# Attention with P times V of two steps in a row, a sixth buffer of exponentials, and scores and merged pieces ordered by array half

## The chip, the cores and the metric

One core of one Trainium2 chip. The metric is the device time of the whole kernel in microseconds, the median of the runs. The core's engines work side by side, each through its own list of instructions in order, and wait for each other on semaphores: TensorE (PE; its weight loads are PEld), VectorE (DVE), ScalarE (ACT), GpSimd (POOL) and SyncE (SP), which issues most DMAs. Matmuls write to PSUM, which has 8 banks of 128 x 512 float32.

## What is computed

Three stages on x of 4 x 1024 x 128: a feed-forward block with 8 experts, causal attention with 16 heads of 8 dimensions over 4 key heads, and the feed-forward block again. The change touches the attention alone:

```python
def _L0_attn_ref(qkv, Wq, bq, Wk, bk, Wv, bv, Wo, bo, slopes):
    ...
    scores = jnp.einsum('bhgqd,bhkd->bhgqk', qg, k) * scale
    rel = jnp.arange(S)[None, :] - jnp.arange(S)[:, None]
    bias = slopes.reshape(KVH, G, 1, 1) * rel
    causal = jnp.tril(jnp.ones((S, S), dtype=bool))
    bias = jnp.where(causal, bias, -jnp.inf)
    attn = jax.nn.softmax(scores + bias[None], axis=-1)
    out = jnp.einsum('bhgqk,bhkd->bhgqd', attn, v)
    ...
    return out @ Wo + bo
...
x = x + 0.5 * _L0_ffn_ref(_layernorm(x), ...)
x = x + _L0_attn_ref(_layernorm(x), ...)
x = x + 0.5 * _L0_ffn_ref(_layernorm(x), ...)
```

## The kernel before

The attention runs over 16 units, a unit being one batch and one key head with its 4 query heads, 1024 queries and 1024 keys. Each unit is done twice over:

- **Row maxima.** For every block of 128 queries and each head the scores q.k + bias are computed as [queries x keys] and VectorE takes the maximum over the keys. This is cut into NP1 = 38 pieces (`PIECES`), each of which fills one PSUM bank: 0 and 1 are merged pieces of 2 products of 256 columns, 2 to 5 of 384 columns, 6 to 9 of 512, 10 and 11 merged pieces of 4 products of 128 columns, 12 to 15 of 512, 16 and 17 merged like 0 and 1, 18 to 21 of 512, 22 to 25 of 384, 26 to 29 of 512, 30 to 37 of 512. A merged piece ends with two mask matmuls. VectorE reduces a piece at line 903 (TENSOR_REDUCE), or at line 896 where it adds the causal mask itself.
- **Softmax and product.** The scores are computed again, transposed, as [keys x queries] with the maximum already subtracted, so that ScalarE only has to take the exponential (line 624), and P times V and the sum of each row come from one float32 matmul per head (`times_v`, below: the product). This runs in NSTEP = 12 steps: (j, kt) with j the half of the queries and kt the block of 128 keys. Steps 0 to 3 have 512, 384, 256 and 128 query columns, 4 to 7 have 512, 8 to 11 have 512, 384, 256 and 128 again.

**The array.** A head's query and key rows (bias rows and products of parts, 57 or 59 of them) lie in partitions 0 to 63 for heads 0 and 1 and in 64 to 127 for heads 2 and 3. So each score matmul uses one half of the array's rows; pieces with an even number are of the lower half, odd ones of the upper. `score(i, s, p)` computes the scores of two heads, one in each half (r = 0 and r = 1), into the banks 3 + 2p and 4 + 2p. A product uses all 128 rows and 32 columns for each of 4 heads, side by side; the trace shows each of its 4 float32 matmuls as two rows, 8 in all.

**Banks.** Pieces, transposed maxima and transposed outputs take turns in a ring of RING = 3 banks: `slot` makes TensorE wait until VectorE has emptied what was put in the ring three places before. The scores have 4 banks, the product one (`OBANK`).

**Order.** `body(i)` works on the softmax and product of unit i, while the pieces of unit i + 1 are threaded through it; the last body has none. In step s TensorE's list is: `PER_STEP[s][0]` pieces; score 0 of step s + 1; `PER_STEP[s][1]` pieces; score 1 of step s + 1; `PER_STEP[s][2]` pieces; the product of step s - LAG (LAG = 2, so steps 10 and 11 of a unit come in steps 0 and 1 of the next body); `PER_STEP[s][3]` pieces; and in some steps the transpose of the maxima (steps 0 and 5) or of the outputs (steps 4 and 6). A score waits for the exponential that last read its banks (one step before, same p), a product for the exponentials of its step. The exponentials of step s go to buffer s modulo PR_BUFS, and ScalarE waits until the product of step s - PR_BUFS is done. In steps 3 and 6 ScalarE also copies the finished output bank (line 613), once that half's last product is done. VectorE's list follows the same order of pieces; it also joins the maxima after pieces 11 and 37 and normalises outputs in steps 4 and 6 (lines 940 and 941). In the first feed-forward block TensorE already computes pieces of unit 0 (`early_pieces`).

Of the kernel before, what the change touches and what calls it, by code (L numbers as in the profile page):

```python
# [12 lines left out]
P = 128  # L13
# [20 lines left out]
K1 = BIAS_ROWS + PRODS  # L34
K2 = K1 + 2
RG = 64
# [13 lines left out]
def pass1_pieces():  # L50
# [8 lines left out]
    for t in (2, 3):  # L59
# [9 lines left out]

PER_STEP = [(2, 1, 0, 0), (0, 1, 1, 0), (0, 2, 2, 1), (0, 2, 0, 0), (0, 3, 0, 0), (0, 2, 0, 1),  # L70
            (0, 3, 1, 1), (1, 0, 2, 1), (0, 2, 0, 1), (0, 2, 0, 0), (1, 0, 2, 0), (2, 1, 0, 0)]
# [9 lines left out]
RING, SBANK, OBANK = 3, 3, 7  # L81
LAG, PR_BUFS = 2, 5

# [92 lines left out]
def macaron(nc, dram, out):  # L176
    ctx = ExitStack()
    with ctx:
# [837 lines left out]
        def _(pe):  # L1016
# [63 lines left out]
            def ffn_down(f, qkv):  # L1080
                def early_pieces(some):
                    for n in some:
                        if n == 0:
                            pe.wait_ge(a_ld[0][0], 16 * LOADS)
                            pe.wait_ge(s_ks0, 4)
                        if n == SECOND_STACK:
                            pe.wait_ge(a_ld[1][0], 16 * LOADS)
                        piece(0, n)

# [63 lines left out]

            def piece(i, n):

                t, h0, per, k0, w, diag = PIECES[n]
                par = i % 2
                at = RG * (h0 // SLOTS)
                b = slot(a_out, NP1 * i + n + 1)
                for k in range(per):  # L1160
                    half, h = k // SLOTS, h0 % SLOTS + k % SLOTS
                    q0, key0 = (t + QT * half) * P, k0 + HALF * half
                    ins = mm(ps[:, b, k * w:k * w + w], qs[at:at + K1, par, q0 // HALF, h, q0 % HALF:q0 % HALF + P],
                             ks[at:at + K1, par, key0:key0 + w], start=k == 0, stop=per == 1)
                if per > 1:
                    o = ps[:, b, 0:per * w].rearrange("p (s n) -> p s n", s=per)
                    mask = mask_qk[at:at + RG, :, None, :].broadcast_to([RG, 2, per, P])
                    mm(o[:, :, w - P:w], spread[at:at + RG, 0, :], mask[:, 0], start=False)
                    ins = mm(o[:, :, w - RG:w], spread[at:at + RG, 1, :], mask[:, 1, :, RG:P], start=False)
                ins.then_inc(a_in, 1)  # L1170

            def maxima_T(i, j):
# [10 lines left out]
            def score(i, s, p, par):  # L1183
# [4 lines left out]
                after(pe, a_ex, NEXP * i + SLOTS * s + p - 1)  # L1188
                for r in range(2):
                    at = RG * r  # L1190
                    ins = mm(ps[:, SBANK + 2 * p + r, lo:HALF], ks[at:at + K2, par, kt * P:(kt + 1) * P],
                             qs[at:at + K2, par, j, p, lo:HALF], stop=not diag)
                if diag:
                    for half, w in enumerate((RG, P)):
                        for r in range(2):
                            rows = slice(RG * r, RG * r + RG)
# [19 lines left out]
            def attention():  # L1216
# [4 lines left out]
                pe.wait_ge(a_ld[1][0], 16 * LOADS)  # L1221
                for n in range(EARLY_END + sum(TAIL), NP1):
                    piece(0, n)
                pe.wait_ge(a_wd[0], 32)
# [3 lines left out]
                def body(i, par, first, last):  # L1228
                    def pieces(s, k):
                        for n in () if last else part(s, k):  # L1230
                            if n == 0:
                                next_stack(i, par, 0)
                            if n == SECOND_STACK:
                                next_stack(i, par, 1)
                            piece(i + 1, n)

                    for s in range(NSTEP):
# [5 lines left out]
                        for p in range(SLOTS):  # L1243
# [4 lines left out]
                            pieces(s, 1 + p)  # L1248
                        if s >= LAG:
                            times_v(i, s - LAG, par)  # L1250
                        elif not first:
                            times_v(i - 1, NSTEP + s - LAG, 1 - par)
                        pieces(s, 3)
# [105 lines left out]
```

## Time and profile before

| | |
|---|---|
| median of 3 runs | 739.92 us (739.89 to 741.77) |
| the profiled execution | 740.43 us, of which the span of its instructions is 738.6 |
| busy over the span | TensorE 702.6 us (95%), VectorE 582.3 (79%), ScalarE 403.3 (55%), GpSimd 112.6 (15%) |
| clock granted to TensorE | 0.972 on average |
| attention | from about 187 us (scores of unit 0) to 600 us; the body without pieces is the last, from about 574 us |

A group below says which view it is. Times are from the start of the span. "Busy" of TensorE counts a matmul until its last result is written, so that pipelined matmuls overlap and a busy TensorE can still be waiting; where one starts is the surer number. An idle time in brackets, or behind the bar, is that of the engine just before the instruction, with what ended it.

### The profile page before, as it was taken

To read this page: it belongs to the slowest core of one execution; us is meant where nothing else is said; L and a number is where in the kernel's file an instruction comes from. 1 tells how busy PE (TensorE), PEld (TensorE's weight loads), DVE (VectorE), ACT (ScalarE), POOL (GpSimd) and SP (SyncE) were. 2 spreads that over 40 slices of the span, in tenths; PEclk is the share of its full clock that TensorE was granted. 3 is DMA by queue.
4 is the path that set the end of the run, shared out by engine and by line. 5 is a ranking of instruction groups with operands and counts; after the bars stand their busy time and mean duration, and the time that the engine had idled before them with its cause. 6 is when DMAs were issued, how large, how long until landed. Compare 5 with 4: busy or idle time off the path is not lost.

```text
span 738.6 us, 15927 instructions
## 1 busy us (share of the span) xinstructions
PE 702.6 (95%) x5906; PEld 365.6 (50%) x5906; DVE 582.3 (79%) x1921; ACT 403.3 (55%) x579; POOL 112.6 (15%) x122
## 2 busy tenths in 40 slices
PE   8999998967999999999999999999999889999998
PEld 4554487833344444444444444444444255554598
DVE  6976468697999999999999999999999238766311
ACT  3353332132667777776777777677777743353300
POOL 3202882110000000000000000000000002103950
PEclk9999999975899999999999999999999999999999
DMA  8014533442010011001100100110010000005531
GB/s 217 1 16 77 93 64 113 144 139 85 25 38 26 27 26 40 20 21 38 33 26 20 39 20 22 39 38 20 21 39 1 2 1 0 2 1 91 107 92 58
DMA packets 47249, 34.69 MB, mean 47 GB/s; under 512 B 13106, under 2 KB 46514, under 8 KB 47172
## 3 DMA queue, kind: packets, MB, share of 16 engines
q1 hardware_dynamic: 46596, 33.60, 18.6%
q8 instruction: 47, 0.77, 0.4%
q14 instruction: 30, 0.25, 0.1%
q10 hardware_dynamic: 576, 0.08, 0.1%
HBM read 23.01 MB, written 10.39 MB: 45 GB/s over the span
## 4 chain that ended last, share of the span: by engine, by line
PE 52%; DVE 13%; issue 11%; ACT 2%; DVEq 0%; ACTq 0%
PE ps L1018 49%; DVE mx L903 8%; PE ps L1023 4%; DVE mx L896 1%; ACT h_all L624 1%; DVE h_all L896 1%; DVE xn L705 1%; DVE stats L693 0%; DVE wb L923 0%; DVE mm_ L920 0%; DVE sg L838 0%; ACT osb L613 0%; DVE idle L894 0%; DVEq L133 0%; DVE mv L697 0%
## 5 line engine op out<-in xcount | busy, mean ns | idle before, releaser
L624 ACT ACTIVATE h_all<-ps 128x1024 f32<-128x1024 f32 (+3 forms) x384 | 291.3, 810 | 112.4 <-PE ps L1018 109.2
L903 DVE TENSOR_REDUCE mx<-ps 128x1 f32<-128x512 f32 (+2 forms) x352 | 223.0, 681 | 9.2 <-PE ps L1018 5.8
L1018 PE MATMUL ps<-ks,xnT_all 57*128 57x512 bf16 (+3 forms) x768 | 178.9, 337 | 15.6 <-DVE mx L896 6.4
L1018 PE MATMUL ps<-h_all,vb 128*32 128x512 f32 (+3 forms) x1536 | 163.8, 500 | 0.6 <-ACT osb L613 0.6
L1018 PE MATMUL ps<-xnT_all,ks 59*128 59x512 bf16 (+3 forms) x768 | 158.6, 331 | 3.6 <-ACT h_all L624 3.4
L896 DVE CUSTOM_DVE_ANT_0 h_all<-ps,mask_w 128x384 bf16<-128x384 f32 (+1 forms) x256 | 149.3, 618 | 2.3 <-issue 0.7
L1018 PEld LDWEIGHTS ps<-ks,xnT_all 57*128 57x128 bf16 x768 | 56.5, 94 | 143.4 <-DVE mx L896 64.9
L1018 PE MATMUL ps<-cb 64*128 64x64 bf16 (+3 forms) x1216 | 113.0, 215 | 0.0
L717 DVE TENSOR_TENSOR h_all<-ps,sg 128x512 f32<-128x512 f32 x80 | 55.2, 690 | 50.5 <-PE ps L1018 48.8
L563 ACT ACTIVATE sg<-ps 128x512 f32<-128x512 f32 x80 | 47.8, 597 | 82.6 <-PE ps L1018 82.3
L1018 PEld LDWEIGHTS ps<-cb 64*128 64x128 bf16 x1216 | 80.1, 96 | 17.3 <-issue 0.7
L1018 PE MATMUL ps<-xnT_all,wg 128*128 128x512 f32 x160 | 83.3, 602 | 0.0
L1018 PE MATMUL ps<-xnT_all,wu 128*128 128x512 f32 x160 | 81.7, 592 | 0.0
L1018 PE MATMUL ps<-wds,h_all 128*128 128x128 f32 x640 | 76.0, 279 | 0.0
L1018 PEld LDWEIGHTS ps<-wds,h_all 128*128 128x128 f32 x640 | 74.0, 194 | 2.7 <-issue 2.7
L1018 PEld LDWEIGHTS ps<-xnT_all,ks 59*128 59x128 bf16 x768 | 45.0, 93 | 42.8 <-ACT h_all L624 26.0
L520 POOL COPY vb<-v_all 128x64 f32<-128x64 f32 x16 | 3.7, 238 | 376.4 <-PE ps L1018 362.0
L1018 PEld LDWEIGHTS ps<-h_all,vb 128*32 128x32 f32 x1536 | 30.5, 108 | 38.1 <-issue 29.2
L1018 PEld LDWEIGHTS ps<-xnT_all,wu 128*128 128x128 f32 x160 | 30.4, 190 | 38.3 <-issue 38.0
L480 POOL TENSOR_TENSOR rstd<-ve,mhalf 128x4 f32<-128x4 f32 x24 | 24.2, 1009 | 151.6 <-DVE ve L699 145.0
L1018 PEld LDWEIGHTS ps<-xnT_all,wg 128*128 128x128 f32 x160 | 28.9, 190 | 28.7 <-issue 28.7
L858 DVE TENSOR_TENSOR x<-x,ps 128x512 f32<-128x512 f32 x16 | 10.9, 683 | 34.0 <-PE ps L1018 34.0
(120 smaller groups left out, 553.6 us busy)
## 6 DMA issues: line engine op xcount, KB each, us to landing
xnT_all<-q_scr SPq DMA_DIRECT2D x64, 96.0 KB
attn<-sel_scr SPq DMA_DIRECT2D x12, 256.0 KB, 7.2
mask_second<-sel_scr SPq DMA_DIRECT2D x12, 256.0 KB, 8.2
q_scr<-qp SPq DMA_DIRECT2D x8, 384.0 KB
ks<-k_scr SPq DMA_DIRECT2D x64, 48.0 KB
x<-in_x SPq DMA_DIRECT2D x8, 256.0 KB, 5.7
yT<-sel_scr SPq DMA_DIRECT2D x8, 256.0 KB, 9.0
q_scr<-qp SPq DMA_DIRECT2D x8, 256.0 KB
```

What stands on the lines that cost most here:

```text
L480: pool.tensor_tensor(rstd[:, par, :], ve[:, par, :], mhalf[:, :], ALU.pow).then_inc(rs_sem, 1)
L520: pool.tensor_copy(vb[:, par, :, 0:DH], v_all[:, i, :, :]).then_inc(a_vb, 1)
L563: act.activation(sg[:, b, :], bank(3 + b), ACT.Silu).then_inc(f.sg, 1)
L624: act.activation(pr[:, (NSTEP * i + s) % PR_BUFS, p:HPG:SLOTS, lo:HALF], ps[:, b:b + 2, lo:HALF], ACT.Exp)\
L705: ins = dve.tensor_scalar(xn[:, t, :], x[:, c * GT + t, :], mv[:, par, t, 0:1], rstd[:, par, t:t + 1], V.subtract, V.mult)
L717: dve.tensor_tensor(h_all[:, TILE_ORDER[k][0], TILE_ORDER[k][1], :], bank(5 + b), sg[:, b, :], V.mult)\
L858: dve.tensor_tensor(xt(c), xt(c), y, V.add).then_inc(f.x, 1)
L896: dve.tensor_tensor_reduce(out=junk, in0=ps[:, b, 0:w], in1=mask_w[:, HALF - w:HALF], scale=1.0, scalar=LOWEST, op0=V.add, op1=V.max, accu ...
L903: dve.tensor_reduce(m, src, AX.X, V.max).then_inc(a_out, 1)
L1018: return pe.matmul(o, l, r, start=start, stop=stop, skip_group_check=True)
L1023: ins = pe.transpose(ps[:, b, t * P:(t + 1) * P], src(t), ident)
```

## The change

Four things, all in the attention:

1. `PER_STEP[5]` is (0, 1, 0, 2) instead of (0, 2, 0, 1): piece 16 moves behind the product and stands with 17.
2. The products of two steps are issued in a row, at odd steps only: steps s - 3 and s - 2 at step s. Even steps have none. There are six buffers of exponentials instead of five.
3. Two merged pieces of the same shape that stand together in a step (0 and 1, 10 and 11, 16 and 17) are issued as one (`two_pieces`): TensorE takes both banks first, then issues their matmuls in turn, one of each half, and signals both at the end.
4. `score` issues first the half that the last piece did not use, then the other. `RowsUsed.last` notes that half while the program is built.

```diff
--- before.py
+++ after.py
@@ -67,7 +67,7 @@
 FIRST_HALF = sum(t < QT for t, *_ in PIECES)
 SECOND_STACK = PIECES.index((0, 0, 4, 0, P, True))
 
-PER_STEP = [(2, 1, 0, 0), (0, 1, 1, 0), (0, 2, 2, 1), (0, 2, 0, 0), (0, 3, 0, 0), (0, 2, 0, 1),
+PER_STEP = [(2, 1, 0, 0), (0, 1, 1, 0), (0, 2, 2, 1), (0, 2, 0, 0), (0, 3, 0, 0), (0, 1, 0, 2),
             (0, 3, 1, 1), (1, 0, 2, 1), (0, 2, 0, 1), (0, 2, 0, 0), (1, 0, 2, 0), (2, 1, 0, 0)]
 assert sum(map(sum, PER_STEP)) == NP1 and len(PER_STEP) == NSTEP
 
@@ -79,7 +79,7 @@
 
 
 RING, SBANK, OBANK = 3, 3, 7
-LAG, PR_BUFS = 2, 5
+LAG, PR_BUFS = 2, 6
 
 BO_PARTS = 8
 WARM_FIRST, WARM_SECOND = 3, 5
@@ -1079,13 +1079,12 @@
 
             def ffn_down(f, qkv):
                 def early_pieces(some):
-                    for n in some:
-                        if n == 0:
-                            pe.wait_ge(a_ld[0][0], 16 * LOADS)
-                            pe.wait_ge(s_ks0, 4)
-                        if n == SECOND_STACK:
-                            pe.wait_ge(a_ld[1][0], 16 * LOADS)
-                        piece(0, n)
+                    if 0 in some:
+                        pe.wait_ge(a_ld[0][0], 16 * LOADS)
+                        pe.wait_ge(s_ks0, 4)
+                    if SECOND_STACK in some:
+                        pe.wait_ge(a_ld[1][0], 16 * LOADS)
+                    pieces_of(0, some)
 
                 def down(c, par, transpose=False):
                     pe.wait_ge(f.hm, MASK_PARTS * (c + 1))
@@ -1151,23 +1150,52 @@
                     pe.wait_ge(*ring.emptied[n - RING])
                 return b
 
-            def piece(i, n):
+            class RowsUsed:
+                last = 1
+
+            def piece_products(i, n, b):
 
                 t, h0, per, k0, w, diag = PIECES[n]
                 par = i % 2
                 at = RG * (h0 // SLOTS)
-                b = slot(a_out, NP1 * i + n + 1)
                 for k in range(per):
                     half, h = k // SLOTS, h0 % SLOTS + k % SLOTS
                     q0, key0 = (t + QT * half) * P, k0 + HALF * half
-                    ins = mm(ps[:, b, k * w:k * w + w], qs[at:at + K1, par, q0 // HALF, h, q0 % HALF:q0 % HALF + P],
+                    yield mm(ps[:, b, k * w:k * w + w], qs[at:at + K1, par, q0 // HALF, h, q0 % HALF:q0 % HALF + P],
                              ks[at:at + K1, par, key0:key0 + w], start=k == 0, stop=per == 1)
                 if per > 1:
                     o = ps[:, b, 0:per * w].rearrange("p (s n) -> p s n", s=per)
                     mask = mask_qk[at:at + RG, :, None, :].broadcast_to([RG, 2, per, P])
-                    mm(o[:, :, w - P:w], spread[at:at + RG, 0, :], mask[:, 0], start=False)
-                    ins = mm(o[:, :, w - RG:w], spread[at:at + RG, 1, :], mask[:, 1, :, RG:P], start=False)
+                    yield mm(o[:, :, w - P:w], spread[at:at + RG, 0, :], mask[:, 0], start=False)
+                    yield mm(o[:, :, w - RG:w], spread[at:at + RG, 1, :], mask[:, 1, :, RG:P], start=False)
+                RowsUsed.last = h0 // SLOTS
+
+            def piece(i, n):
+
+                b = slot(a_out, NP1 * i + n + 1)
+                for ins in piece_products(i, n, b):
+                    pass
                 ins.then_inc(a_in, 1)
+
+            def two_pieces(i, n):
+
+                upper, lower = slot(a_out, NP1 * i + n + 1), slot(a_out, NP1 * i + n + 2)
+                for first, second in zip(piece_products(i, n, upper), piece_products(i, n + 1, lower)):
+                    pass
+                first.then_inc(a_in, 1)
+                second.then_inc(a_in, 1)
+                RowsUsed.last = PIECES[n + 1][1] // SLOTS
+
+            def pieces_of(i, some):
+
+                n = some.start
+                while n < some.stop:
+                    together = n + 1 < some.stop and PIECES[n][2] > 1 and PIECES[n][2:] == PIECES[n + 1][2:]
+                    if together:
+                        two_pieces(i, n)
+                    else:
+                        piece(i, n)
+                    n += 2 if together else 1
 
             def maxima_T(i, j):
                 b = slot(a_wc, 2 * i + j + 1)
@@ -1186,13 +1214,14 @@
                 lo = max(0, kt - QT * j) * P
                 diag = kt >= QT * j
                 after(pe, a_ex, NEXP * i + SLOTS * s + p - 1)
-                for r in range(2):
+                order = (1 - RowsUsed.last, RowsUsed.last)
+                for r in order:
                     at = RG * r
                     ins = mm(ps[:, SBANK + 2 * p + r, lo:HALF], ks[at:at + K2, par, kt * P:(kt + 1) * P],
                              qs[at:at + K2, par, j, p, lo:HALF], stop=not diag)
                 if diag:
                     for half, w in enumerate((RG, P)):
-                        for r in range(2):
+                        for r in order:
                             rows = slice(RG * r, RG * r + RG)
                             ins = mm(ps[:, SBANK + 2 * p + r, lo:lo + w], spread[rows, half, :],
                                      mask_kq[rows, half, 0:w], start=False)
@@ -1219,20 +1248,19 @@
                     pe.wait_ge(a_ld[half][1 - par], 8 * LOADS * (i + 3 if par else i + 2))
 
                 pe.wait_ge(a_ld[1][0], 16 * LOADS)
-                for n in range(EARLY_END + sum(TAIL), NP1):
-                    piece(0, n)
+                pieces_of(0, range(EARLY_END + sum(TAIL), NP1))
                 pe.wait_ge(a_wd[0], 32)
                 for p in range(SLOTS):
                     score(0, 0, p, 0)
 
                 def body(i, par, first, last):
                     def pieces(s, k):
-                        for n in () if last else part(s, k):
-                            if n == 0:
-                                next_stack(i, par, 0)
-                            if n == SECOND_STACK:
-                                next_stack(i, par, 1)
-                            piece(i + 1, n)
+                        some = range(0) if last else part(s, k)
+                        if 0 in some:
+                            next_stack(i, par, 0)
+                        if SECOND_STACK in some:
+                            next_stack(i, par, 1)
+                        pieces_of(i + 1, some)
 
                     for s in range(NSTEP):
                         pieces(s, 0)
@@ -1246,10 +1274,11 @@
                             elif not last:
                                 score(i + 1, 0, p, 1 - par)
                             pieces(s, 1 + p)
-                        if s >= LAG:
-                            times_v(i, s - LAG, par)
-                        elif not first:
-                            times_v(i - 1, NSTEP + s - LAG, 1 - par)
+                        for done in (s - LAG - 1, s - LAG) if s % 2 else ():
+                            if done >= 0:
+                                times_v(i, done, par)
+                            elif not first:
+                                times_v(i - 1, NSTEP + done, 1 - par)
                         pieces(s, 3)
                         if s == W1_STEP:
                             maxima_T(i, 1)
```

## Rows read from the trace of the kernel before

**Rows 1.** Busy time of each engine by stretch: the attention, and one body

```profile
core 0: us, PE busy (x) PEld busy (x) DVE busy (x) ACT busy (x) POOL busy (x), PEclk, DMA share, GB/s
187.00:574.00 387.00, 380.38 (x4160) 164.67 (x4163) 371.87 (x1216) 286.53 (x390) 11.85 (x21) 0.99 0.10 27
...
394.98:420.68 25.70, 25.26 (x282) 10.95 (x279) 24.71 (x81) 19.10 (x27) 0.24 (x1) 1.00 0.11 28
```

**Rows 2.** Chain of work that ended last: start, duration, what; one period

```profile
418.28 2.41 DVE mx L903 x4
424.82 5.12 PE ps L1018 x46
...
443.99 2.41 DVE mx L903 x4
```

**Rows 3.** Groups of instructions, 300 to 500 us: busy, mean ns | idle before

```profile
L624 ACT ACTIVATE h_all<-ps 128x1024 f32<-128x1024 f32 x95 | 92.1, 1024 | 35.5 <-PE ps L1018 35.1
...
L1018 PE MATMUL ps<-h_all,vb 128*32 128x512 f32 x376 | 50.1, 605 | 0.0
```

**Rows 4.** Waits, 300 to 500 us: us in total, times, longest

```profile
PEld ps L1018 <- DVE mx L896: 30.0, 38, 0.8
...
DVE mx L903 <- PE ps L1018: 2.5, 10, 0.3
```

**Rows 5.** Timeline of VectorE, step 6's end to step 8: start, duration

```profile
410.96 0.29 DVE L941 TENSOR_TENSOR attn<-ps,rden 128x128 f32<-128x128 f32 x1
...
412.63 0.08 DVE L896 DVE_READ_ACCUMULATOR2_ANT mx<- 128x1 f32 x1
412.99 1.89 DVE L903 TENSOR_REDUCE mx<-ps 128x1 f32<-128x512 f32 x3 [0.28 <-PE ps L1018]
415.03 0.69 DVE L903 TENSOR_REDUCE mx<-ps 128x1 f32<-128x512 f32 x1 [0.15 <-PE ps L1018]
```

**Rows 6.** Timeline of TensorE, step 7: piece 25, a product, piece 26

```profile
411.31 0.33 PE L1018 MATMUL ps<-ks,xnT_all 57*128 57x384 bf16 x1
411.57 1.06 PE L1018 MATMUL ps<-h_all,vb 128*32 128x512 f32 x8
412.57 0.39 PE L1018 MATMUL ps<-ks,xnT_all 57*128 57x512 bf16 x1
```

**Rows 7.** Timeline of TensorE, products of unit 15's steps 8, 9, 10, three windows

```profile
596.12 2.36 PE L1018 MATMUL ps<-h_all,vb 128*32 128x512 f32 x32
...
597.00 1.48 PE L1018 MATMUL ps<-h_all,vb 128*32 128x384 f32 x24
...
597.65 0.83 PE L1018 MATMUL ps<-h_all,vb 128*32 128x256 f32 x16
```

**Rows 8.** Timeline of TensorE, step 5: piece 16's masks and score 1

```profile
405.34 0.39 PE L1018 MATMUL ps<-xnT_all,ks 59*128 59x512 bf16 x1
405.44 0.33 PE L1018 MATMUL ps<-cb 64*128 64x256 bf16 x2
405.61 0.38 PE L1018 MATMUL ps<-xnT_all,ks 59*128 59x512 bf16 x1
```

**Rows 9.** Timeline of TensorE, step 3: pieces 10 (from 400.66) and 11

```profile
400.66 0.39 PE L1018 MATMUL ps<-ks,xnT_all 57*128 57x128 bf16 x4
...
400.98 0.34 PE L1018 MATMUL ps<-ks,xnT_all 57*128 57x128 bf16 x3
401.11 0.27 PE L1018 MATMUL ps<-cb 64*128 64x256 bf16 x1
```

**Rows 10.** Timeline of TensorE in the last body: a wait, scores, a product

```profile
586.84 0.39 PE L1018 MATMUL ps<-xnT_all,ks 59*128 59x512 bf16 x2 [1.01 <-ACT h_all L624]
587.16 1.88 PE L1018 MATMUL ps<-h_all,vb 128*32 128x512 f32 x8
```

**Rows 11.** Timeline of VectorE: pieces 34 to 37, then the next body's piece 0

```profile
418.20 2.48 DVE L903 TENSOR_REDUCE mx<-ps 128x1 f32<-128x512 f32 x4
...
421.23 0.68 DVE L903 TENSOR_REDUCE mx<-ps 128x2 f32<-128x512 f32 x1
```

## The prediction

> **What bounds the kernel now.** I read the busy times by stretch first, then the chain of work that ended last, the groups of instructions, the waits, and last the timelines of VectorE and TensorE over one body. The attention stretch fills 387 of the 738.6 us, and TensorE and VectorE both count as nearly full there [rows 1]. Within it one pattern returns: the chain meets the same four VectorE reductions at 418.28 and at 443.99, 25.7 us apart [rows 2]. That is one body (one unit's softmax and product, with the next unit's row maxima threaded through it), and 15 bodies carry maxima; the sixteenth doesn't. In a body VectorE is busy 24.71 of 25.70 us and ScalarE 19.10 [rows 1], and over 200 us VectorE waits only 2.5 us for TensorE while TensorE's weight loads wait 30 us for VectorE's line 896 alone [rows 4]. So VectorE sets the pace: three banks stand between the engines, and TensorE refills one as soon as VectorE empties it.
>
> Where VectorE does wait tells what binds it. Four times per body it waits visibly, always just behind a product. Piece 25 goes to TensorE at 411.31, 0.06 us after VectorE emptied its bank (410.96 + 0.29) [rows 5, 6]; the product takes 411.57 to 412.57, then piece 26 is computed, and VectorE, free since 412.71, starts on it at 412.99 (the profile counts 0.28 of idle; a back-to-back reduction would have started near 412.63, so the loss is 0.36) [rows 5, 6]. The next product costs 0.23: three reductions take 1.89, so they stand 0.60 apart and a fourth could start at 414.80; it starts at 415.03 [rows 5]. Counted in this way, start against the possible start, a body loses about 1.3 us, so VectorE's own work is 24.4 us. That 1.3 us, 19 us over 15 bodies, is all that any relief of TensorE can win here.
>
> **The change, part by part.** Times are per body unless said.
>
> *Changes of mode saved.* A full product occupies TensorE 1.00 us up to the next work (411.57 to 412.57) [rows 6]. In the last body products follow each other directly, and a full one takes 0.88 (596.12 to 597.00) and one of 384 columns 0.65 [rows 7]. So leaving product form costs 0.11; entering costs 0.09 (piece 25 streams 384 columns, 0.16, behind 411.31, and the product begins 0.10 later) [rows 6]. Pairing removes six products from even steps. Steps 2, 6, 8 and 10 save two changes each, step 4 one (a transpose of outputs follows it), step 0 none, since the transpose of maxima, of the same form, now enters alone. Nine changes at 0.1 are 0.9 us of TensorE's time.
>
> *What two products in a row do to VectorE.* TensorE works in program order, so nothing for VectorE is computed during a pair. The ring holds three banks, at most 1.8 us of reductions (3 x 0.60), whatever lead TensorE had before. A full pair holds it 1.88, and with the last piece's stream, the scores and the next piece's own latency the gap is 2.5 to 3.1 us. I set each pair's gap against the work VectorE still has:
> - Steps 4 and 5, in step 7: exactly the place of [rows 5, 6], where the ring was already full and 0.36 already lost. One more product in front of piece 26 adds 0.88. Step 6, now without a product, gives back the 0.16 that VectorE waited there. Net +0.70.
> - Steps 6 and 7, in step 9: piece 31 is issued 0.06 behind a reduction; VectorE has 1.70 left. Gap: stream 0.21, scores 0.20, entry 0.09, pair 1.88, latency of piece 32 0.42 (412.57 to 412.99 [rows 5, 6]), 2.80. Loss 1.10, against 0.09 there and 0.23 in step 8 before. Net +0.78.
> - Steps 8 and 9, in step 11: VectorE has three reductions and the joining of the maxima. Four reductions and the join take 3.03 (418.20 to 421.23 [rows 11]), so 2.29 is left behind the issue of piece 37. Gap 0.21 + 0.30 + 0.09 + 1.53 + 0.11 + 0.59 = 2.83. Net +0.54.
> - Steps 0 and 1, in step 3: from the start of pieces 10 and 11 to piece 12 it is 0.54 + 0.22 + 0.09 + 1.53 + 0.11 + 0.22 + 0.42 = 3.13; VectorE reaches 12 after 2.38. Loss 0.75 against 0.17 before. Net +0.58.
> - Steps 2 and 3, in step 5: short products (0.43 + 0.25), but pieces 16 and 17 now both stand behind them. From piece 15's issue to 16 being ready 2.02, work left 1.36; loss 0.66 against 0.11. Net +0.55. It rests on the second score waiting for ScalarE, whose exponentials take 1.02 each [rows 3] and start later behind the pair of step 3; without that it is +0.2.
> - Steps 10 and 11, in step 1: 0.68 of product between pieces 4 and 5, where 0.25 stood. +0.4, or +0.76 if scores come late as above; I take +0.6.
>
> *Merged pieces in twos.* A merged piece no longer starts when its own bank is empty, but when the second's is too, one reduction later. For pieces 10 and 11 VectorE has 0.48 of work left then, and the piece takes 0.71 (400.66 to 401.11 + 0.27) [rows 9] plus 0.04: +0.27. For 0 and 1 and for 16 and 17 it is inside the sums above. The interleaving wins nothing: piece 11's products already run before piece 10's last mask (400.98 against 401.11) [rows 9].
>
> *Scores ordered by half.* Taken at nothing. The score of step 6 is written lower half first, behind piece 16, which is in the lower half. In the trace one of its two matmuls starts at 405.34, before piece 16's masks at 405.44, and the other at 405.61 [rows 8]: the upper half's already went ahead. Bounds: no gain, to 0.21 (one stream) at seven places, 1.5 us.
> The Trainium skill says otherwise: by "TensorE: Matmul & The Clock Gate" (Part 3, The mechanism) matmuls start and end strictly in program order and only weight loads overtake. By it the new order would shorten the stream by up to the 1.5 us just named, and the forecast would be 22 us lower; the trace disagrees, by 405.34 before 405.61.
>
> *Six buffers of exponentials.* Nothing is lost or won: a product now comes up to one step later, and the sixth buffer gives ScalarE that step. ScalarE has 6.6 us per body to spare [rows 1]. If it had no cover, exponentials would wait for the pair, which my sum for step 5 bounds.
>
> **Sum.** Pieces 10/11 and the pairs in steps 3, 5, 7, 9 act in all 15 bodies: (0.27 + 0.58 + 0.55 + 0.70 + 0.78) x 15 = 43.2. Those in steps 11 and 1 act between two bodies, 14 times: 1.14 x 14 = 16.0. The last body has no maxima; TensorE and ScalarE carry it. It starts 0.9 later behind the pair of step 11 and regains about as much, because scores no longer stand behind a product that waits for ScalarE: 0. The rest of the kernel (351 us) is untouched but for two early pieces: 0. In all +59 us on the profiled execution's 740.4 (738.6 of span), 0.5 above the median of 739.9: 800 us, a body of 29.8 us. A difference above 0.3% is what a measurement can tell here.
>
> **Rivals.**
> *Faster.* The 0.9 us of changes reach VectorE instead of being overrun by its starving. For it: its waits all stand behind products. It decides at a gap no longer than the ring's cover, 1.8 us: then the waits shrink, by 0.9 x 15, to 727, at best by 1.3 x 15, to 721. Against it: with one product the gap at 411.31 to 412.99 is 1.68, and VectorE already loses 0.36. Chance 0.08. The skill's rule on order belongs here: alone it doesn't turn the sign.
> *A smaller loss.* Only the four pairs with full products cost what I say, and the small terms (10/11, steps 5 and 1) vanish: (0.58 + 0.70 + 0.78) x 15 + 0.54 x 14 = 38.5, so 779; with 1 us per body regained elsewhere, 765. Chance 0.14.
> *The clock falls too.* TensorE would wait some 4 us more per body. In the last body, after waits of up to 1.01 us, eight product rows take 1.88 instead of 1.06 [rows 6, 10], the lower of the two levels (1.2 against 2.4 GHz). If one full pair per body ran so, 1.9 x 15 = 28 more: 828; for part of the bodies 812 and up. Against it: the pairs themselves keep TensorE at work, and the attention stretch has 0.99 granted now [rows 1]. Chance 0.12.
> *It makes no difference*, because the ends overlap in a way no row shows: within 0.3%, chance 0.02.
>
> **How the numbers follow.** My forecast, with 785 to 812 for errors of about 0.9 us in a body's 4, has 0.62; others 0.02 (slower). With most of the smaller loss and half of the clock's case the range is 766 to 824. Faster 0.08, same 0.02, slower 0.90.
>
> **What would show it.** Right: the pattern of the chain returns after 29 to 30 us; VectorE's busy time stays near 24.7 per body while its waits for TensorE rise to about 5, the longest near 1.0 us before pieces 26 and 32; eight product rows become sixteen with 0.9 between the two; TensorE's waits for VectorE in steps without products grow. Wrong: reductions that run on through a pair, a piece's matmul that starts inside one, a body at or under 25.7, or a granted clock well under 0.99.

## The result and the profile after

| | before | changed |
|---|---|---|
| median | 740.6 us | 839.45 us (835.28 to 843.2) |
| ratio to before | | 1.134, 95% interval 1.130 to 1.139 |
| profiled execution, its span | 740.4, 738.6 us | 835.3, 833.5 us |
| clock granted to TensorE, mean | 0.972 | 0.934 |

The change costs 99 us; I had forecast 59, and 824 as the end of the range. The direction and the starving of VectorE were right; the size wasn't, because a second cost, the clock, had been taken for unlikely. The clock is the first thing that the page of the changed kernel shows. These are its slices, each a fortieth of the span; the digits of a row are busy tenths, for PEclk the granted clock:

```profile
DVE  6974487878787877788767878767878704858311
...
PEclk9999999859999989998979999879999899999999
```

VectorE (DVE), nines through all of the attention before, is at 6 to 8. The granted clock, 9 in every slice from the twelfth on before, now dips again and again to 7 or 8. Stretches of the changed kernel (columns as in [rows 1]): one body at full clock, the body that the clock hit hardest, and most of the attention.

```profile
219.06:248.95 29.89, 25.96 (x282) 11.14 (x280) 24.74 (x81) 19.32 (x26) 1.46 (x2) 1.00 0.09 24
...
538.25:572.47 34.22, 30.48 (x282) 12.25 (x280) 24.89 (x81) 19.32 (x26) 0.24 (x1) 0.85 0.09 24
...
219.00:600.00 381.00, 334.71 (x3300) 139.17 (x3294) 294.62 (x964) 229.93 (x310) 11.41 (x19) 0.92 0.08 22
```

VectorE's work is the 24.7 us of [rows 1] in either body. With the clock at its upper level throughout, a body takes 29.89 us instead of 25.70; where 0.85 was granted on average it takes 34.22. TensorE is idle for 3.9 us of the first body (29.89 less 25.96), against 0.4 before. The same 219 to 600 us of the kernel before had 1.00 granted.

Groups of the changed kernel, 300 to 500 us (against [rows 3]), and its waits there (against [rows 4]):

```profile
L903 DVE TENSOR_REDUCE mx<-ps 128x1 f32<-128x512 f32 x100 | 62.4, 680 | 23.9 <-PE ps L1018 23.9
...
L1018 PE MATMUL ps<-h_all,vb 128*32 128x512 f32 x320 | 47.9, 709 | 0.0
```
```profile
DVE mx L903 <- PE ps L1018: 31.9, 31, 3.1
...
DVE h_all L896 <- issue: 12.0, 16, 1.0
```

A reduction still takes 680 ns, but VectorE's waits for TensorE went from 2.5 us to 31.9, the longest from 0.3 to 3.1. Another 12.0 us of idle, up to 1.0 at a time, now stand in front of line 896; the profile names no releaser for them ("issue"). A row of the product went from 605 to 709 ns on average. In pairing alone, below, where the clock falls in few bodies, it is 609 in the same stretch, so the rise is the clock's and not the pair's.

The place of [rows 5, 6] in a body at full clock, first TensorE from piece 25 on, then VectorE:

```profile
236.83 0.33 PE L1018 MATMUL ps<-ks,xnT_all 57*128 57x384 bf16 x1
237.10 1.92 PE L1018 MATMUL ps<-h_all,vb 128*32 128x512 f32 x16
238.95 0.39 PE L1018 MATMUL ps<-ks,xnT_all 57*128 57x512 bf16 x1
```
```profile
238.15 0.08 DVE L896 DVE_READ_ACCUMULATOR2_ANT mx<- 128x1 f32 x1
239.38 2.48 DVE L903 TENSOR_REDUCE mx<-ps 128x1 f32<-128x512 f32 x4 [1.14 <-PE ps L1018]
```

Sixteen product rows stand where eight stood, and the next piece's matmul starts 1.85 us after the first of them instead of 1.00. VectorE's idle grew from 0.28 to 1.14. This is the starving that the prediction drew. Its other side is step 2 of the same body, TensorE's timeline, where a product stood before and none does now:

```profile
223.34 0.39 PE L1018 MATMUL ps<-ks,xnT_all 57*128 57x512 bf16 x1 [0.30 <-DVE mx L896]
223.96 0.39 PE L1018 MATMUL ps<-ks,xnT_all 57*128 57x512 bf16 x1 [0.23 <-DVE mx L896]
224.06 0.51 PE L1018 MATMUL ps<-xnT_all,ks 59*128 59x512 bf16 x2
225.29 0.40 PE L1018 MATMUL ps<-ks,xnT_all 57*128 57x128 bf16 x8 [0.72 <-DVE mx L896]
```

TensorE idles between pieces, 0.30, 0.23 and 0.72 us, with its three banks full. Step 6 is its twin, with waits of 0.30, 0.21, 0.21 and 0.26. In this body the clock held. In the next one the same wait of 0.72 stands at the same place, and from there the clock is at its lower level (TensorE's timeline, then the stretch behind it; 0.50 is 1.2 of 2.4 GHz):

```profile
255.18 0.61 PE L1018 MATMUL ps<-ks,xnT_all 57*128 57x128 bf16 x8 [0.72 <-DVE mx L896]
```
```profile
255.12:258.52 3.40, 3.34 (x26) 1.18 (x30) 2.18 (x6) 1.48 (x2) 0.00 (x0) 0.50 0.03 5
```

All falls in the bodies with pieces begin in or just behind steps 2 and 6, 6.2 to 7.0 or 15.7 to 17.2 us into the body, and then catch the next pair. A pair of full products at the lower level, TensorE and VectorE in the worst body:

```profile
560.70 1.84 PE L1018 MATMUL ps<-h_all,vb 128*32 128x512 f32 x8
562.47 0.39 PE L1018 MATMUL ps<-ks,xnT_all 57*128 57x512 bf16 x1
```
```profile
562.89 2.48 DVE L903 TENSOR_REDUCE mx<-ps 128x1 f32<-128x512 f32 x4 [3.02 <-PE ps L1018]
```

These are the second eight rows of the pair: 1.77 us to the next piece instead of 1.00, and VectorE waits 3.02.

Not every body pays. The first two take 29.4 and 29.9 us. From 249 us on they take 31.5 and 32.6, then 31.5, 31.2, 32.7 and 34.2 over and over, each with one or two falls, though their pieces, scores and products are the same.

**The account.** From the first to the last reduction of maxima VectorE takes about 92 us longer. At full clock the 15 bodies lose 3.6 (the first), 13 x 4.19 and 3.6 (the last with pieces), 61.7 in all. Every body's excess over that, read from the starts of its reductions, adds 30.4: the clock. Behind them the last body, without pieces, lost 1.8 and the rest of the kernel 1.2, together 95 between the two profiled executions. The median lies 4 us further, for the granted clock of the changed kernel wanders between runs, from 0.917 to 0.934.

### The profile page after: what moved, and what is told of

It is laid out like the page before. It is cut to its first block, busy times and chain, and to the rows that moved or that the text cites. A ratio compares the mean times of both kernels' runs of the same rounds, so it can differ in the third digit from the quotient of the medians.

```text
span 833.5 us, 15941 instructions
## 1 busy us (share of the span) xinstructions
PE 743.0 (89%) x5906; PEld 377.4 (45%) x5906; DVE 583.9 (70%) x1921; ACT 406.6 (49%) x579; POOL 112.8 (14%) x122
## 4 chain that ended last, share of the span: by engine, by line
PE 47%; issue 17%; DVE 15%; ACT 1%; DVEq 0%; ACTq 0%
PE ps L1018 43%; DVE mx L903 10%; PE ps L1023 4%; DVE mx L896 2%; ACT h_all L624 1%; DVE h_all L896 1%; DVE xn L705 1%; DVE stats L693 0%; DVE idle L894 0%; DVE wt L912 0%; DVE sg L838 0%; DVEq L133 0%; ACT osb L613 0%; DVE mv L697 0%; DVE qp L841 0%
## 5 line engine op out<-in xcount | busy, mean ns | idle before, releaser
L624 ACT ACTIVATE h_all<-ps 128x1024 f32<-128x1024 f32 (+3 forms) x384 | 294.4, 810 | 201.0 <-PE ps L1018 198.3
L1018 PE MATMUL ps<-ks,xnT_all 57*128 57x512 bf16 (+3 forms) x768 | 189.1, 344 | 50.4 <-DVE mx L896 28.8
L1018 PE MATMUL ps<-xnT_all,ks 59*128 59x512 bf16 (+3 forms) x768 | 160.4, 343 | 12.7 <-ACT h_all L624 12.0
L1018 PEld LDWEIGHTS ps<-ks,xnT_all 57*128 57x128 bf16 x768 | 53.8, 95 | 162.4 <-DVE mx L896 59.7
L1018 PEld LDWEIGHTS ps<-h_all,vb 128*32 128x32 f32 x1536 | 42.5, 116 | 74.1 <-issue 55.8
L1018 PEld LDWEIGHTS ps<-xnT_all,wu 128*128 128x128 f32 x160 | 30.4, 190 | 38.3 <-issue 38.0
L705 DVE TENSOR_SCALAR xn<-x,mv,rstd 128x128 f32<-128x128 f32 x96 | 33.7, 415 | 5.2 <-POOL rstd L480 5.0
```

The costliest lines, as they stand in the source:

```text
L624: act.activation(pr[:, (NSTEP * i + s) % PR_BUFS, p:HPG:SLOTS, lo:HALF], ps[:, b:b + 2, lo:HALF], ACT.Exp)\
L705: ins = dve.tensor_scalar(xn[:, t, :], x[:, c * GT + t, :], mv[:, par, t, 0:1], rstd[:, par, t:t + 1], V.subtract, V.mult)
L1018: return pe.matmul(o, l, r, start=start, stop=stop, skip_group_check=True)
```

## The experiments

Ratios are to the kernel before, run on the same chip beside each. "Body" is the distance between the starts of piece 0's reduction in a body where the clock stayed at its upper level.

**Pairing alone.** The kernel before with these two edits.

```diff
-LAG, PR_BUFS = 2, 5
+LAG, PR_BUFS = 2, 6
...
-                        if s >= LAG:
-                            times_v(i, s - LAG, par)
-                        elif not first:
-                            times_v(i - 1, NSTEP + s - LAG, 1 - par)
+                        for done in (s - LAG - 1, s - LAG) if s % 2 else ():
+                            if done >= 0:
+                                times_v(i, done, par)
+                            elif not first:
+                                times_v(i - 1, NSTEP + done, 1 - par)
```

> The kernel before with only the pairing of the products and the sixth buffer; old order of pieces, scores and merged pieces. Theory (the pair starves VectorE, and the lull in the steps without a product drops TensorE's clock): bodies of 29.2 to 29.8 us where the clock is full, because pieces 10 and 11 no longer cost 0.27 extra, granted clock 0.92 to 0.94, 820 to 840 us. Rival (the grouping by halves and of merged pieces is what costs): 740 us, clock 0.97.

Measured: 805.7 us, ratio 1.089 (1.086 to 1.092), body 29.69 us. The body is as expected, the clock isn't: it fell in only three of the fifteen bodies. So the pairing costs 65 us, of which the three falls are 4.3, and something else in the change brings most of the clock's loss.

```profile
278.63:308.32 29.69, 26.79 (x282) 11.74 (x280) 24.65 (x81) 19.21 (x26) 1.46 (x2) 1.00 0.09 25
219.00:600.00 381.00, 344.19 (x3528) 150.46 (x3524) 312.92 (x1031) 244.63 (x330) 11.62 (x20) 0.99 0.08 24
```

**Grouping alone.** The changed kernel with a product in every step, five buffers and the old `PER_STEP` (the diff above turned round, and the change's first two hunks).

> The changed kernel with the products back at every step, five buffers and the old place of piece 16; only scores and merged pieces ordered by half stay. Theory: merged pieces wait for two banks, +0.3 us per body, score order nothing: 743 to 746 us, clock 0.97. Rival one (matmuls run strictly in program order, so the order by halves saves up to 1.5 us of TensorE per body, of which VectorE can take 1.3): 721 to 735. Rival two (the order is the cause of the slowdown): above 800.

Measured: 741.5 us, ratio 1.002 (1.0005 to 1.004), body 25.86 us, 0.15 more than before. Read piece by piece, piece 10 starts 0.33 late and piece 12 makes up 0.17; no other reduction moves by over 0.01. So the merged pair costs what was expected, half of it is made up, and the order of the scores does nothing. The time is 1.5 us under the range that I had given, for the same reason. The gain that strict program order would promise isn't there.

**Idle work in all even steps.** Added to the changed kernel.

```diff
+            def filler(i, s, par):
+
+                j, kt = STEPS[s]
+                after(pe, a_ex, NEXP * i + SLOTS * s - 1)
+                for _ in range(4):
+                    for r in range(2):
+                        at = RG * r
+                        mm(ps[:, SBANK + r, :], ks[at:at + K2, par, kt * P:(kt + 1) * P],
+                           qs[at:at + K2, par, j, 0, :])
...
+                            if p == 0 and s % 2 == 0:
+                                filler(i, s + 1, par)
```

> The changed kernel with idle work for TensorE in the even steps: before the first score of the next step, eight matmuls of 512 columns (four in each half, 0.86 us) into the banks that this score then overwrites. Nothing of the result changes. Theory (the clock falls because TensorE is too little at work in the steps without a product): the granted clock in the attention is back at 0.98 or more and the time at 795 to 808 us, bodies 29.9 to 30.3. Rival (the clock falls because of the pair's burst itself, or of something else): clock still 0.92 there and 835 to 850 us.

Measured: 869.2 us, ratio 1.174, body 33.91 us. The clock came back (1.00 from 219 to 600 us, with one fall, in one body of 35.52), the time didn't: the idle work stood in front of the first score and of the pieces behind it, where VectorE was already starved, so it delayed pieces 3, 5, 12, 27 and 33 by 0.5 to 0.9 each. It speaks for the cause, but not for the price. It also says what the cause is not: TensorE is idle for 4.0 us of such a body (33.91 less 29.92), as long as in the changed kernel, and keeps its clock. What differs is the work that stands between the waits.

**Idle work in steps 2 and 6 only**, before the second score and behind freshly issued pieces.

```diff
+                            if p == 1 and s in (2, 6):
+                                filler(i, s + 1, par)
```

with the filler writing to the second pair of score banks (`SBANK + 2 + r`), behind a wait for the exponential that last read them.

> The changed kernel with the idle work (eight matmuls of 512 columns, 0.86 us) only in steps 2 and 6 and ahead of the second score, where pieces have just been issued, so that it hardly delays VectorE. Theory (the clock falls after the lulls of steps 2 and 6): granted clock in the attention 0.98 or more, bodies of 29.9 to 30.4, 798 to 810 us. Rival (the fall has other causes): 835 us or more with clock 0.92.

Measured: 806.6 us, ratio 1.090 (1.083 to 1.098), body 30.01 us, and no fall of the clock from 219 us to the last body with pieces:

```profile
219.62:249.64 30.02, 26.81 (x298) 12.43 (x296) 24.82 (x81) 19.44 (x26) 1.46 (x2) 1.00 0.09 27
219.00:600.00 381.00, 340.08 (x3737) 158.00 (x3735) 314.85 (x1031) 247.48 (x330) 11.63 (x20) 1.00 0.09 24
```

Sixteen matmuls more per body, whose result nobody reads, make the changed kernel 33 us faster. This is the clock's share, taken away nearly by itself (the body is 0.12 us longer), and it shows the cause: too little work for TensorE in these two of the steps that lost their product. The pairs' bursts are all still there. No run put the same sixteen matmuls into other steps, so that only steps 2 and 6 would do is not shown.

**The pair split by pieces.** In odd steps the pieces of the fourth place go between the two products.

```diff
-PER_STEP = [(2, 1, 0, 0), (0, 1, 1, 0), (0, 2, 2, 1), (0, 2, 0, 0), (0, 3, 0, 0), (0, 1, 0, 2),
-            (0, 3, 1, 1), (1, 0, 2, 1), (0, 2, 0, 1), (0, 2, 0, 0), (1, 0, 2, 0), (2, 1, 0, 0)]
+PER_STEP = [(2, 1, 0, 0), (0, 1, 0, 1), (0, 2, 2, 1), (0, 0, 0, 2), (0, 3, 0, 0), (0, 1, 0, 2),
+            (0, 3, 1, 1), (1, 0, 1, 2), (0, 2, 0, 1), (0, 1, 0, 1), (1, 0, 2, 0), (2, 0, 0, 1)]
...
-                        for done in (s - LAG - 1, s - LAG) if s % 2 else ():
+                        for n, done in enumerate((s - LAG - 1, s - LAG) if s % 2 else ()):
+                            if n == 1:
+                                pieces(s, 3)
...
-                        pieces(s, 3)
+                        if s % 2 == 0:
+                            pieces(s, 3)
```

> The changed kernel with the pieces of the fourth place between the two products of an odd step, and one or two pieces moved to that place in steps 1, 3, 7, 9 and 11 (two stand there in step 5 already). Lag, buffers, order by halves and number of products per step stay; only the two products no longer stand side by side. Theory (the gap between pieces is what costs): bodies of 26 to 28 us, 750 to 780 us. Rival (the later products, the sixth buffer or the late output copies cost): above 800.

Measured: 816.3 us, ratio 1.103, body 29.70 us; the clock fell in ten of the fifteen bodies. My expectation failed: that the two stand side by side isn't what costs. In step 9 piece 31, now between the products, starts 0.72 late and piece 32 another 0.61, together 1.33, where the unbroken pair cost 1.02 in front of 32. One piece between two products brings VectorE 0.6 us of work while each product takes 1.00 from entry to exit; and the changes of mode, two more per pair, are back. As I read it, what counts is that two products, 2.0 us of TensorE's time, come within one step, while the three banks hold 1.8 us of work for VectorE. It isn't a clean test of that: pieces also moved within five steps, which has costs and gains of its own (0.67 more in front of piece 4, 0.78 less in front of 12).

**Lateness without pairs.** The kernel before with

```diff
-LAG, PR_BUFS = 2, 5
+LAG, PR_BUFS = 3, 6
...
-OT0_STEP = 6
+OT0_STEP = 7
```

> The kernel before with each product one step later (three steps behind its exponentials instead of two), six buffers, and the transpose of the first outputs in step 7 instead of 6; one product in every step. Theory (it is the gathering of two products in one step that costs): 738 to 748 us, bodies of 25.7 to 26.2. Rival (the later products, output copies and normalisations cost, which the split pair left open): bodies of 28 us or more, above 775.

Measured: 763.8 us, ratio 1.032 (1.025 to 1.039), body 26.95 us. Neither number was met. One product per step, all a step later, costs 1.25 us per body by itself, in amounts of 0.08 to 0.55 in front of pieces 5, 12, 15, 17, 24, 27 and 29, less 0.67 in front of 23, from where the normalisation moved away. Over fifteen bodies that is 19 us; the clock falls in three of them, which adds about 5. As I read it, the products were laid where the pieces leave room, and one step on they meet other pieces and scores. Against the pair's 4.0 it is small. How much of it is in those 4.0 can't be read off, for a pair has one product on its old step and one a step later.

**Two banks.** The kernel before with

```diff
-RING, SBANK, OBANK = 3, 3, 7
+RING, SBANK, OBANK = 2, 3, 7
```

> The kernel before with a ring of two banks instead of three, nothing else changed. Theory (a product costs VectorE what the gap between two pieces exceeds the reductions still in the ring): the cover falls by one reduction, 0.6 us, so each of the four waits behind a product grows by about 0.6 and places with less slack than that begin to wait: bodies of 28.5 to 31.5 us, 785 to 840 us. Rival (the ring is not what limits; the pair costs through the order alone): under 760 us.

Measured: 869 us (one run), body 32.88 us, more than expected. In front of pieces 3, 9, 22, 29, 32 and 35, each the first behind a product, the reduction comes 0.61 to 0.76 later: one reduction's worth, as the cover theory says. There were more such places than I had counted, and the rest of the 7.2 us is spread over pieces 11, 12, 15 to 18, 26 and the next body's 0. And the clock fell here too, in step 6 of every second body, which then takes 35.4 us (0.95 granted from 219 to 660 us). This kernel has a product in every step and no pair; TensorE is idle for 5.3 us of a body (32.87 less 27.54), in eleven of the twelve steps. So a step without its product is one way to lose the clock, not the only one.

**Short products.** Exponentials and V in bf16 for the product; the same edit to the kernel before and to the changed one. It lowers the precision of P times V. The zeros and ones that `vb` was filled with are set in `vb16`.

```diff
-        pr = h_all[:, 0:PR_BUFS, 0:HPG, :]
+        pr = h_all[:, 0:PR_BUFS, 0:HPG, :].bitcast(BF16)[:, :, :, 0:HALF]
+        vb16 = sb("vb16", [P, 2, SEQ // P, 32], BF16)
...
-                pool.tensor_copy(vb[:, par, :, 0:DH], v_all[:, i, :, :]).then_inc(a_vb, 1)
+                pool.tensor_copy(vb16[:, par, :, 0:DH], v_all[:, i, :, :]).then_inc(a_vb, 1)
...
-                    ins = mm(ps[32 * h:32 * h + 32, OBANK, lo:HALF], vb[:, par, kt, :],
+                    ins = mm(ps[32 * h:32 * h + 32, OBANK, lo:HALF], vb16[:, par, kt, :],
```

> The kernel before with exponentials and V in bf16 for the product alone, so that a product of 512 columns takes one pass, 0.22 us, instead of 0.88 (this lowers the precision of P times V). Theory (VectorE waits only behind products): its 1.3 us of waits per body mostly go, bodies of 24.4 to 24.9, 720 to 730 us, unless the clock falls for lack of work, then 730 to 750. Rival (VectorE's waits come from scores or ScalarE): 738 to 742.

Measured: 719.1 us, ratio 0.972 (0.962 to 0.981), body 24.30 us. The first group is the main kind of reduction, 300 to 500 us:

```profile
L905 DVE TENSOR_REDUCE mx<-ps 128x1 f32<-128x512 f32 x134 | 83.6, 679 | 0.0
```

No idle time is left in front of it. A full product now takes 0.34 us up to the next work, from 302.75 to the start of the next piece's matmul at 303.09, against 1.00:

```profile
302.75 0.40 PE L1020 MATMUL ps<-h_all,vb 128*32 128x512 bf16 x4
```

The body is the 24.4 us that the prediction had given as VectorE's own work, to 0.1. The interval of the ratio reaches from 4% to 2% faster.

> The changed kernel with exponentials and V in bf16 for the product alone. Theory (length of the pair against the cover of three banks): a pair is now 0.45 us, shorter than one float32 product, so VectorE is not starved: within 1% of the kernel before in bf16, bodies of 24.5 to 25.4, 720 to 745 us. Rival (late products, ScalarE's waits or the merged pieces cost the 4 us per body): bodies of 28 us or more, above 775.

Measured: 737.5 us in one execution and 758.2 in the other, with mean clocks of 0.942 and 0.902. The first is 2.6% above the kernel before in bf16, not within the 1% that I expected. It has bodies of 24.98 us at full clock and of 26.2 in every second body, where the clock falls. So with short products all of the change costs 0.68 us per body at full clock instead of 4.19: its price hangs on the length of the pair. And the clock falls here, in step 6 of every second body, where the kernel before with the same short products keeps it in every body from 214 to 553 us (its 0.957 over the whole span comes from a fall of 44 us around the start of the attention and one of 14 in the last body). TensorE's matmuls are the same in both, bunched or spread; it is idle for 4.1 us of a body here (24.98 less 20.89) and for 1.5 there (24.30 less 22.81).

**Which part tips the clock.** Three kernels, each the changed one with one part undone.

```diff
-                    if together:
-                        two_pieces(i, n)
-                    else:
-                        piece(i, n)
-                    n += 2 if together else 1
+                    piece(i, n)
+                    n += 1
```

> The changed kernel with merged pieces issued one by one again; paired products, six buffers, score order and the new place of piece 16 stay. Theory (the two-bank wait of pieces 10 and 11 lengthens the lull of step 2, which tips the clock): bodies at full clock 29.6, granted clock in the attention 0.97 or more, 803 to 815 us. Rival (the score order or the place of piece 16 tips it): clock 0.92, 828 to 840 us.

Measured: 816.2 us, ratio 1.101, body 29.80 us, clock 0.958 over the span. That is just outside what I had expected of the theory, and far from the rival's numbers. The clock no longer falls behind step 2, but in every third body it still does in step 6. At full clock the joint issue costs only 0.09 us per body: without it piece 10 comes 0.36 earlier and piece 12 waits 0.27 more.

```diff
-                order = (1 - RowsUsed.last, RowsUsed.last)
+                order = (0, 1)
```

> The changed kernel with scores in the old order, lower half first. Theory (the array reorders by itself, and the score order does nothing): bodies at full clock 29.9, clock 0.92, 833 to 843 us. Rival (the score order packs TensorE's work and so makes the lulls): clock above 0.96, 800 to 815 us.

Measured: 845.0 us (843.4 and 846.6), ratio 1.140, clock 0.913. Its bodies repeat the changed kernel's own pattern (31.5, 31.2, 32.7, 34.2 us). The time is 2 us above my range, and its interval (1.132 to 1.147) overlaps that of the changed kernel. The order of the scores has no part in it, as expected.

```diff
-PER_STEP = [(2, 1, 0, 0), (0, 1, 1, 0), (0, 2, 2, 1), (0, 2, 0, 0), (0, 3, 0, 0), (0, 1, 0, 2),
+PER_STEP = [(2, 1, 0, 0), (0, 1, 1, 0), (0, 2, 2, 1), (0, 2, 0, 0), (0, 3, 0, 0), (0, 2, 0, 1),
```

> The changed kernel with piece 16 back in front of the pair of step 5; merged pieces 16 and 17 then are not issued together. Theory (the place of 16 is one of several places that load step 5): bodies at full clock 29.8 to 29.9, and the clock as in the changed kernel, 0.92, 830 to 843 us. Rival (it is this place that tips the clock): 803 to 815 us, clock above 0.97.

Measured: 816.2 us, ratio 1.101, body 29.78 us, clock 0.954. Against my expectation this place matters as much as the merged pairs. So two changes that cost under 0.2 us each at full clock cost some 20 us each through it. Undoing either wins 23 us, and without both and the score order (pairing alone) 34. So small differences in TensorE's waits go with large ones in the clock. They can't be the whole of it: bodies of one kernel with the same work lose the clock in some cases and keep it in others, in a fixed order (every third body without joint issue, every second with short products, the four of the changed kernel). What decides between equal bodies is not shown here, and so it stays open whether these two edits act through their tenths of waiting alone or through when in time the waits come.

## Why the prediction fell short

**The pairs: right, and to a tenth.** The starts of the reductions in a body at full clock give each term of the sum:

| term | forecast | measured |
|---|---|---|
| steps 10 and 11, in step 1 | 0.6 | 0.68 |
| pieces 10 and 11 issued together | 0.27 | 0.36 |
| steps 0 and 1, in step 3 | 0.58 | 0.61 |
| steps 2 and 3, in step 5 | 0.55 | 0.56 |
| steps 4 and 5, in step 7 | 0.70 | 0.67 |
| steps 6 and 7, in step 9 | 0.78 | 0.79 |
| steps 8 and 9, in step 11 | 0.54 | 0.57 |
| body at full clock | 29.8 | 29.89 |

The terms of the forecast add up to 4.02, so to a body of 29.72; the prediction rounds it up. The line on pieces 10 and 11 is no price of its own: issued one by one, they leave 0.27 of its 0.36 to the pair of step 3, and the joint issue costs 0.09.

The method was to set the gap between two pieces against the reductions still in the ring, both from rows. Its image of the cause held under test: a shorter product takes the cost away, a shorter ring brings it to single products. One thing it got by luck: I wrote as if the two products had to be adjacent, and the split pair costs as much.

**The changes of mode saved: right that they win nothing.** A full pair takes 1.85 us to the next piece where two single products took 2.00, so the saving is there (over a body it was not measured). VectorE doesn't see it: at even steps TensorE waits for it anyway, and what VectorE gets back there, 0.19 in front of piece 23 and 0.23 in front of 29, are the waits behind the products that left, which the forecast had counted.

**The order by halves: right, nothing** [rows 8]. Two kernels show it, one without pairs and one with them. The sign of overtaking is that a score starts at 405.34, before the masks at 405.44 that stand ahead of it in the program, and not the pair of times that the prediction names last, 405.34 and 405.61, which are the two scores.

**The last body: a little short**, 1.8 us instead of 0, from its last reduction of maxima to its last normalisation.

**The clock: the step that failed.** I had it as a rival at 0.12, priced 28 us, and it took 30.4 in the profiled execution, about 34 at the median. The chance was wrong. The price was near the mark, in part by luck: it was one pair per body at the lower level, 1.9 us in each of 15, and what came was 1.3 to 4.3 us in each of 13 bodies and nothing in two. The argument against it was that "the pairs themselves keep TensorE at work". They do, but the clock fell in and behind steps 2 and 6, which had lost their product, and these I had looked at only for what they give VectorE. There the prediction also said that TensorE would wait some 4 us more per body, and [rows 10] showed what this kernel does after a wait of 1.01. I had both numbers and read the first as spread over the body. It came as 3.9 us of idle, and over half of it stands in steps 2 and 6 (1.25 and 0.98), where two scores and one piece per reduction are all that is left for TensorE. With this rival as part of the forecast, 740 + 4.2 x 15 + 30, the sum would have been 833.

The range failed with it: it ended at 824, with half of the rival's case inside, while the sum of forecast and rival in full was 828, and the truth above.

## What to carry to other kernels

When two engines share a ring of n banks, the longest block that the producer can put between two deliveries without starving the consumer is n of the consumer's steps (three banks, 1.8 us, here); work that doesn't feed the consumer is best cut small and spread, even if each cut costs a change of mode. Where work is moved out of a step, ask two questions of the step it leaves: who had been covered by it, and does TensorE still have enough to do there to keep its clock. In this kernel edits worth a tenth of a microsecond per body moved the total by 23 us through the clock, so a change should be priced at both clock levels.

## What the runs showed of the hardware

- Less work alone didn't lose the clock. The kernel before with short products (0.34 us instead of 1.00) keeps it in every body from 214 to 553 us with TensorE busy for 94% of a body, while the same work in pairs, 84% busy, loses it in every second body.
- Nor does the idle time alone tell: 4.0 us per body kept the clock with idle work added in six steps (one fall), 3.9 lost it in 13 of 15 bodies of the changed kernel, and 5.3 spread over eleven steps lost it in every second body with two banks.
- Matmuls that nobody reads can pay: 16 per body in steps 2 and 6 gave back 33 us; 48 per body in front of the first scores of all even steps kept the clock as well, and cost 30 us.
- Matmuls of the two row halves don't keep program order between them [rows 8, 9]; writing the scores in the better order changed no start of a reduction by more than 0.01 us (pieces 10 and 12 aside, which the joint issue moved).
- The fastest version found is the kernel before with bf16 exponentials and V, 719.1 us against 740.7, where VectorE's own work is all that is left of a body. It computes P times V at lower precision.
